# Three PSUM banks each for scores and transposed scores, with key sums moved behind the weighted product, in a differential-attention and gated-FFN kernel

## The chip, the cores and the metric

The kernel runs on one core of a Trainium2 chip. The metric is the device time of one execution in microseconds; times below are of the whole program, from the first to the last instruction unless said otherwise.

## The reference

The input is x, 16 batch elements of 1024 tokens with 256 features, float32. Cut to what matters:

```python
# x: (16, 1024, 256); H = 8 heads, D = 16, two score maps per head
n = layernorm(x)
q, k = xpos_rope(n @ Wq.T), xpos_rope(n @ Wk.T)     # 16 maps of depth 16
v = n @ Wv.T                                         # 8 heads of depth 32
probs = softmax(q @ k.T / 4)                         # 16 maps of 1024 x 1024
attn = (probs[:, 0] - lam * probs[:, 1]) @ v
x = x + (rms_norm(attn) * KEEP) @ Wo.T
n = layernorm(x)
c = scan over the batch: c = sigmoid(n@wf.T + c@uf.T + bf) * c
                           + sigmoid(n@wi.T + c@ui.T + bi) * tanh(n@wc.T + c@uc.T + bc)
out = x + tanh(n @ wo.T + c_final @ uo.T + bo)
```

The scan runs over the 16 batch elements, so the gates of one element need the cell state of the one before; the output needs the last cell state, so it is computed in a tail behind all elements.

## The kernel before, in words

The five engines run lists of instructions of their own and wait for each other's semaphores. The order on each engine is written out by hand. `iteration(b)` handles one batch element: the next element's queries and keys, the attention of two groups of four heads (attention 0 and attention 1), the mean squares and the output projection, the second normalisation, and the gates.

**Attention, in `attention`.** Each of the two attentions has 32 steps. In a step TensorE makes four transposed score tiles (`key_tile`, line 777: 128 keys by 512 queries of each of four heads, bf16, a row of the maxima added in the same product). ScalarE turns them into probabilities (`exps`, line 564). The probabilities are float32 and are used in two ways: the weighted product with the values (`weighted`, line 792, into `o_ps`), and the sums over the keys, the softmax denominators. For these POOL adds the probabilities of two successive steps (`pair`, line 472, one instruction per head), and TensorE multiplies the pair's sum by ones (`key_sums`, line 807, into `sum_ps`). Both products write 32 partitions per head, four heads side by side, and each shows as 8 matmuls. `weighted` of step s-1 stands in step s; `key_sums` of pair q, steps 2q and 2q+1, stands in step 2q+4.

**Scores.** The maxima that the softmax needs are taken from untransposed scores: 128 matmuls per attention (`score`, line 749), each into a bank `s_ps` of 512 float32, which VectorE reduces at once (`maximum`, line 1043). They belong to the *next* attention, and a plan (`score_plan`, from an assumed cost of the rotary work and of the sum steps) deals them out over the steps, 0 to 5 per step; 28 and 32 of them stand outside the steps, in the next queries and keys, the projections and the gates.

**PSUM.** It has eight banks. Before, `st[0]` and `st[1]` are two banks each and hold the transposed tiles of heads 0, 1 and 2, 3; `s_ps[0]`, `s_ps[1]` hold scores; `o_ps` and `sum_ps` have one each. A score waits until the maximum two before it is taken (line 748). A pair of tiles waits for the exp of the same half a step earlier (line 774). The ring of all other products (projections, mean squares, gates) goes through the four `st` banks in turn; `turn` is TensorE's wait for a free one, `take` ScalarE's read of it.

**VectorE** has, beside the maxima, the rotary embedding of the next queries and keys (`rope`, in the steps listed in `ROPE_AT`: the first nine and 13, 16 of attention 0; 5 to 10, 12, 13, 16, 20 of attention 1, here called the rotary steps), the turning and inversion of the key sums (`finish_sums`: for the last quarter of attention 0 it stands ahead of the first maximum in attention 1; for the others in steps 11, 19, 27 with `combine` a step later), and the normalisations.

**probs** is a ring of four steps. The exps of step s wait for `weighted` of step s-4 and, in even steps, for POOL's pair of steps s-4 and s-3 (lines 560, 561). POOL waits for all exps of both steps of its pair (line 466).

**Gates.** 12 gate tiles per element, each with a part from the old cell state and one from the normalised rows (line 891). Those of the first four tiles that need only the cell state stand ahead of the transposes of the second normalisation, whose statistics VectorE makes meanwhile (lines 983 to 1008).

The order inside a step, before:

```python
key_tile(u, g, s, 0)          # two tiles, heads 0 and 1
for i in todo[0:1]: score(un, 1 - g, i)
key_tile(u, g, s, 1)          # heads 2 and 3
for i in todo[1:2]: score(un, 1 - g, i)
if s >= 1: weighted(u, g, s - 1)
for i in todo[2:4]: score(un, 1 - g, i)
if s >= 4 and s % 2 == 0: key_sums(u, g, (s - 4) // 2)
for i in todo[4:]: score(un, 1 - g, i)
```

## Time and profile before

| what | us |
|---|---|
| median of three runs | 5261.81 (5261.59 to 5262.73) |
| the profiled execution | 5259.74 |
| its span, first to last instruction | 5257.9 |
| TensorE matmuls busy | 4979.5 (95%) |
| VectorE busy | 4021.4 (76%) |
| POOL busy | 2891.7 (55%) |
| ScalarE busy | 2722.8 (52%) |
| scores, line 749: 4096 matmuls | 1525.8 |
| transposed tiles, line 777: 4096 matmuls | 1226.9 |
| weighted product, line 792: 8192 matmuls | 1103.6 |
| key sums, line 807: 4096 matmuls | 543.4 |

One element takes about 313 us. Matmuls are pipelined and their ends are modelled, so TensorE's busy time overlaps itself; how far apart two matmuls start is the better measure of what each costs.

### The profile page before, as it was taken

Reading aid. Unit: us, or ns where it says so; the run is one execution under the profiler, and the core shown is the slowest. Engines: PE = TensorE matmul, PEld = TensorE weight load, DVE = VectorE, ACT = ScalarE, POOL = GpSimd, SP = SyncE. Lnnn points to the kernel's source line nnn. Section 1 sums busy time; section 2 is a strip of 40 time slices with the busy share of each in tenths; the row PEclk is TensorE's granted clock in tenths of the full one; section 3 lists DMA queues with packets and bytes.
Section 4 is the critical chain, followed back from the end, with each engine's and each line's share of the span. In section 5 each row is a group of like instructions: output and inputs, shape, how many; then the busy total and the mean of one; then the engine's idle time right before and its main releaser. Section 6 shows DMA issues by size and latency. Waiting matters only on the chain.

```text
span 5257.9 us, 65030 instructions
## 1 busy us (share of the span) xinstructions
PE 4979.5 (95%) x24784; PEld 1695.8 (32%) x24784; DVE 4021.4 (76%) x6183; ACT 2722.8 (52%) x3173; POOL 2891.7 (55%) x2118
## 2 busy tenths in 40 slices
PE   6999999999999999999999999999999999999999
PEld 2224232332423223242332423233242322323237
DVE  6877777877778877777887777787777887777526
ACT  1464645556465554545556454554546555463652
POOL 3573746647275573727657374664727557372750
PEclk7899999999999999999999999999999999999999
DMA  6031221302222131222303122130222213122117
GB/s 141 26 60 46 50 64 37 69 37 58 52 45 69 33 64 40 45 66 51 67 26 62 45 45 69 34 72 37 54 56 45 69 33 61 43 45 59 65 49 280
DMA packets 127706, 311.05 MB, mean 59 GB/s; under 512 B 27297, under 2 KB 30498, under 8 KB 113442
## 3 DMA queue, kind: packets, MB, share of 16 engines
q1 hardware_dynamic: 124178, 289.33, 23.2%
q10 hardware_dynamic: 3216, 17.57, 0.9%
q8 instruction: 195, 3.19, 0.3%
q14 instruction: 117, 0.96, 0.1%
HBM read 172.07 MB, written 99.61 MB: 52 GB/s over the span
## 4 chain that ended last, share of the span: by engine, by line
PE 64%; DVE 16%; issue 13%; POOL 3%; ACT 3%; DMA 0%; ACTq 0%; POOLq 0%; SPq 0%; DVEq 0%
PE o_ps L792 15%; PE s_ps L749 15%; PE st L777 13%; PE sum_ps L807 8%; DVE neg_max L1043 7%; PE st L891 3%; PE st L735 3%; POOL pair_sum L472 2%; PE st L717 2%; PE st L957 2%; ACT probs L564 2%; DVE stats L983 2%; DVE xa L1026 1%; DVE swapped L1021 1%; PE st L870 1%
## 5 line engine op out<-in xcount | busy, mean ns | idle before, releaser
L472 POOL TENSOR_TENSOR pair_sum<-probs 128x512 f32<-128x512 f32 x2048 | 2795.4, 1398 | 1436.4 <-ACT probs L564 1432.2
L1043 DVE TENSOR_REDUCE neg_max<-s_ps 128x1 f32<-128x512 f32 x4096 | 2679.4, 687 | 817.4 <-PE s_ps L749 810.1
L564 ACT ACTIVATE probs<-st 128x1024 f32<-128x1024 f32 x2048 | 1983.6, 1022 | 1240.9 <-PE st L777 996.0
L749 PE MATMUL s_ps<-k_stack,q_stack 96*128 96x512 bf16 x4096 | 1525.8, 393 | 140.9 <-DVE neg_max L1043 122.7
L777 PE MATMUL st<-q_stack,k_stack 99*128 99x512 bf16 x4096 | 1226.9, 385 | 20.2 <-ACT xa L512 6.6
L792 PE MATMUL o_ps<-probs,values 128*32 128x512 f32 x8192 | 1103.6, 611 | 0.7 <-ACT probs L564 0.7
L749 PEld LDWEIGHTS s_ps<-k_stack,q_stack 96*128 96x128 bf16 x4096 | 371.1, 97 | 1524.3 <-DVE neg_max L1043 1260.6
L777 PEld LDWEIGHTS st<-q_stack,k_stack 99*128 99x128 bf16 x4096 | 348.3, 99 | 792.6 <-ACT probs L564 414.8
L807 PE MATMUL sum_ps<-pair_sum,ones 128*32 128x512 f32 x4096 | 543.4, 602 | 7.7 <-POOL pair_sum L472 5.7
L891 PE MATMUL st<-xt,weights 128*128 128x512 f32 x768 | 381.7, 594 | 11.8 <-ACT xt L521 11.8
L891 PE MATMUL st<-cell_t,weights 128*128 128x512 f32 x768 | 362.9, 592 | 0.0
L512 ACT ACTIVATE probs<-st,gate_bias 128x512 f32<-128x512 f32 x192 | 131.6, 685 | 429.5 <-PE st L891 429.5
L792 PEld LDWEIGHTS o_ps<-probs,values 128*32 128x32 f32 x8192 | 161.9, 108 | 409.1 <-issue 381.3
L478 POOL TENSOR_TENSOR rstd<-var_eps,neg_half 128x8 f32<-128x8 f32 x18 | 29.6, 1647 | 433.5 <-DVE var_eps L1002 433.5
L717 PE MATMUL st<-xt,weights 128*128 128x512 f32 x512 | 248.1, 604 | 11.0 <-ACT xt L521 11.0
L1070 DVE STREAM_TRANSPOSE attn_t<-sum_ps 128x512 f32<-128x512 f32 x128 | 90.8, 709 | 184.7 <-PE sum_ps L807 184.7
L521 ACT ACTIVATE xt<-o_ps 128x512 f32<-128x512 f32 x64 | 38.2, 597 | 367.7 <-PE o_ps L704 367.6
L891 PEld LDWEIGHTS st<-xt,weights 128*128 128x128 f32 x768 | 144.6, 190 | 138.9 <-issue 113.3
L891 PEld LDWEIGHTS st<-cell_t,weights 128*128 128x128 f32 x768 | 144.6, 190 | 129.2 <-issue 120.8
L512 ACT ACTIVATE xa<-st 128x512 f32<-128x512 f32 x128 | 76.1, 597 | 208.1 <-PE st L717 199.9
L484 POOL TENSOR_TENSOR next_rstd<-var_eps,neg_half 128x8 f32<-128x8 f32 x14 | 22.9, 1636 | 273.2 <-DVE var_eps L1002 273.2
L807 PEld LDWEIGHTS sum_ps<-pair_sum,ones 128*32 128x32 f32 x4096 | 90.4, 108 | 219.2 <-issue 151.3
(129 smaller groups left out, 2980.3 us busy)
## 6 DMA issues: line engine op xcount, KB each, us to landing
q_stack<-qk_parts SPq DMA_DIRECT2D x384, 128.0 KB, 4.3
k_stack<-qk_parts SPq DMA_DIRECT2D x378, 128.0 KB, 7.0
swapped<-xa SPq DMA_DIRECT2D x128, 256.0 KB, 2.4
qk_parts<-swapped SPq DMA_DIRECT2D x64, 512.0 KB, 2.8
xa<-in_x SPq DMA_DIRECT2D x16, 1024.0 KB, 6.1
qk_parts<-low_part SPq DMA_DIRECT2D x64, 256.0 KB, 3.0
probs<-in_x SPq DMA_DIRECT2D x16, 1024.0 KB, 10.2
x_rows<-probs SPq DMA_DIRECT2D x16, 1024.0 KB, 3.9
```

What stands on the lines that cost most here:

```text
L472: pool.tensor_tensor(pair_sum[q % 2][:, h, :], probs[a % 4][:, h, :], probs[(a + 1) % 4][:, h, :], ALU.add)\
L512: act.activation(dst, ring(i), func, **kw).then_inc(act_out, 1)
L564: act.activation(probs[kk % 4][:, 2 * hp:2 * hp + 2, :], st[hp][:, :, :], ACT.Exp).then_inc(exp_done, 1)
L717: mm = pe.matmul(ring(i), weights[:, W_Q + X, c, g * P:(g + 1) * P], xt[:, c, h * HALF:(h + 1) * HALF], start=(c == 0), stop=(c == KC - 1))
L735: mm = pe.matmul(dst, src[:, c, at:at + P], weights[:, w, c, :], start=(c == 0), stop=(c == KC - 1))
L749: pe.matmul(s_ps[i % 2][:, :], q_stack[g][0:SROWS, s, t * P:(t + 1) * P], k_stack[g][0:SROWS, s, h * HALF:(h + 1) * HALF], start=True, sto ...
L777: mm = pe.matmul(st[hp][:, j, :], k_stack[g][0:KROWS, s, kt * P:(kt + 1) * P], q_stack[g][0:KROWS, s, th * HALF:(th + 1) * HALF], start=Tr ...
L792: mm = pe.matmul(o_ps[32 * h:32 * h + 32, :], values[:, kt, at:at + 2 * D], probs[kk % 4][:, h, :], start=(kt == 0), stop=(kt == KT - 1))
L807: mm = pe.matmul(sum_ps[32 * h:32 * h + 32, :], ones[:, 0:32], pair_sum[q % 2][:, h, :], start=(p == 0), stop=(p == 3))
L891: mm = pe.matmul(ring(GATE + i), weights[:, (U_F if cell else W_F) + a, c, ms], (cell_t if cell else xt)[:, c, hs], start=(start and c == ...
L957: mm = pe.matmul(ring(j)[:, t * E:(t + 1) * E], columns[:, at:at + P], weights[:, W_Z, c, :], start=(c == 0), stop=(c == KC - 1))
L1043: dve.tensor_reduce(neg_max2[:, at, i % 2:i % 2 + 1], s_ps[i % 2][:, :], AX.X, ALU.max, negate=True).then_inc(max_done, 1)
```

## The change

The eight banks are dealt out anew: three banks `st` of one tile each, three banks `s_ps`, and `o_ps`, `sum_ps` as before.

- `key_tile` makes one tile and waits for the exp three tiles before it; ScalarE runs one ACTIVATE of 512 columns per tile, 4096 instead of 2048 of 1024.
- A score waits for the maximum three before it.
- In a step the order is tile, score, tile, score, tile, weighted product, key sums, tile, the remaining scores.
- POOL waits per head for the exp of that head in the pair's second step.
- The ring of the other products has three banks; `turn` looks three places back. The bank follows from a count that goes on over the elements (`ring(rb + i)`, `bank`), and only three gates' cell parts stand ahead of the second transposes.
- In the tail the fourth bank is `s_ps[2]`.

```diff
-        st = [ctx.enter_context(nc.psum_tensor(f"st{i}", [P, 2, HALF], F32)) for i in range(2)]
-        s_ps = [ctx.enter_context(nc.psum_tensor(f"s_ps{i}", [P, HALF], F32)) for i in range(2)]
+        st = [ctx.enter_context(nc.psum_tensor(f"st{i}", [P, HALF], F32)) for i in range(BANKS)]
+        s_ps = [ctx.enter_context(nc.psum_tensor(f"s_ps{i}", [P, HALF], F32)) for i in range(BANKS)]
...
-        def ring(i):
-            return st[(i % 4) // 2][:, i % 2, :]
+        def ring(n):
+            return st[n % BANKS][:, :]
...
-                pool.wait_ge(exp_done, 64 * u + 4 * q + 4)
...
                 for h in range(4):
+                    pool.wait_ge(exp_done, TILES * u + 8 * q + 4 + (h + 1))
                     pool.tensor_tensor(pair_sum[q % 2][:, h, :], probs[a % 4][:, h, :],
...
-                    for hp in range(2):
-                        act.wait_ge(st_ready, 64 * u + (2 * kk + hp + 1))
-                        act.activation(probs[kk % 4][:, 2 * hp:2 * hp + 2, :], st[hp][:, :, :],
+                    for h in range(4):
+                        n = 4 * kk + h
+                        act.wait_ge(st_ready, TILES * u + n + 1)
+                        act.activation(probs[kk % 4][:, h, :], st[n % BANKS][:, :],
                                        ACT.Exp).then_inc(exp_done, 1)
...
-                p = i - 4
+                p = i - BANKS
...
-                if i >= 2:
-                    pe.wait_ge(max_done, SCORES * u + (i - 1))
-                pe.matmul(s_ps[i % 2][:, :], q_stack[g][0:SROWS, s, t * P:(t + 1) * P],
+                if i >= BANKS:
+                    pe.wait_ge(max_done, SCORES * u + (i - BANKS + 1))
+                pe.matmul(s_ps[i % BANKS][:, :], q_stack[g][0:SROWS, s, t * P:(t + 1) * P],
...
-            def key_tile(u, g, kk, hp):
+            def key_tile(u, g, kk, h):
...
+                n, s = 4 * kk + h, 2 * h + sub
+                if n >= BANKS:
+
+                    pe.wait_ge(exp_done, TILES * u + (n - BANKS + 1))
+                pe.matmul(st[n % BANKS][:, :], k_stack[g][0:KROWS, s, kt * P:(kt + 1) * P],
+                          q_stack[g][0:KROWS, s, th * HALF:(th + 1) * HALF],
+                          start=True, stop=True).then_inc(st_ready, 1)
...
-                    key_tile(u, g, s, 0)
-                    for i in todo[0:1]:
-                        score(un, 1 - g, i)
-                    key_tile(u, g, s, 1)
-                    for i in todo[1:2]:
-                        score(un, 1 - g, i)
+                    for h in range(2):
+                        key_tile(u, g, s, h)
+                        for i in todo[h:h + 1]:
+                            score(un, 1 - g, i)
+                    key_tile(u, g, s, 2)
                     if s >= 1:
                         weighted(u, g, s - 1)
-                    for i in todo[2:4]:
-                        score(un, 1 - g, i)
                     if s >= 4 and s % 2 == 0:
                         key_sums(u, g, (s - 4) // 2)
-                    for i in todo[4:]:
+                    key_tile(u, g, s, 3)
+                    for i in todo[2:]:
                         score(un, 1 - g, i)
...
-                for i in range(4):
+                for i in range(BANKS):
                     turn(GATE + i, b, ab)
                     gate_part(i, True, True, False)
                 transposes(xn2, ln2_out, b, 2 * b + (1 if last else 2))
```

## Rows read from the trace of the kernel before

**Rows 1.** The page, part 1: busy us, share of the span, instructions.

```profile
PE 4979.5 (95%) x24784; PEld 1695.8 (32%) x24784; DVE 4021.4 (76%) x6183; ACT 2722.8 (52%) x3173; POOL 2891.7 (55%) x2118
```

**Rows 2.** Timeline, two steps of attention 0: start, us, engine, line, what, count, [idle before].

```profile
2130.95 0.39 PE L749 MATMUL s_ps<-k_stack,q_stack 96*128 96x512 bf16 x1
2131.17 0.60 PE L777 MATMUL st<-q_stack,k_stack 99*128 99x512 bf16 x2
2131.37 1.99 DVE L1043 TENSOR_REDUCE neg_max<-s_ps 128x1 f32<-128x512 f32 x3 [0.24 <-PE s_ps L749]
...
2131.89 1.94 ACT L564 ACTIVATE probs<-st 128x1024 f32<-128x1024 f32 x2 [2.52 <-PE st L777]
...
2132.26 0.38 PE L749 MATMUL s_ps<-k_stack,q_stack 96*128 96x512 bf16 x1
...
2132.57 1.07 PE L792 MATMUL o_ps<-probs,values 128*32 128x512 f32 x8
...
2133.57 0.39 PE L749 MATMUL s_ps<-k_stack,q_stack 96*128 96x512 bf16 x1
...
2133.90 4.96 POOL L472 TENSOR_TENSOR pair_sum<-probs 128x512 f32<-128x512 f32 x4 [2.35 <-ACT probs L564]
```

**Rows 3.** Timeline, behind attention 1's last step, TensorE.

```profile
2275.97 1.06 PE L792 MATMUL o_ps<-probs,values 128*32 128x512 f32 x8
2276.85 1.04 PE L807 MATMUL sum_ps<-pair_sum,ones 128*32 128x512 f32 x8
2277.82 0.70 PE L735 MATMUL st<-weights,xt 128*128 128x256 f32 x2
```

**Rows 4.** Timeline, start of attention 1.

```profile
2174.04 1.88 DVE L1043 TENSOR_REDUCE neg_max<-s_ps 128x1 f32<-128x512 f32 x3
...
2174.78 0.39 PE L749 MATMUL s_ps<-k_stack,q_stack 96*128 96x512 bf16 x1 [2.68 <-DVE neg_max L1043]
```

**Rows 5.** Timeline, step 20 of attention 0, TensorE.

```profile
2121.95 0.39 PE L749 MATMUL s_ps<-k_stack,q_stack 96*128 96x512 bf16 x1 [0.28 <-DVE neg_max L1043]
...
2122.55 0.39 PE L749 MATMUL s_ps<-k_stack,q_stack 96*128 96x512 bf16 x1 [0.21 <-DVE neg_max L1043]
```

**Rows 6.** Timeline, behind a step of four scores, attention 0.

```profile
2126.71 0.60 PE L777 MATMUL st<-q_stack,k_stack 99*128 99x512 bf16 x2
...
2127.44 0.10 PEld L749 LDWEIGHTS s_ps<-k_stack,q_stack 96*128 96x128 bf16 x1 [0.63 <-DVE neg_max L1043]
```

**Rows 7.** Timeline, the rotary steps of the next element's attention 0.

```profile
2372.99 27.33 POOL L472 TENSOR_TENSOR pair_sum<-probs 128x512 f32<-128x512 f32 x16 [43.08 <-ACT probs L564]
...
2380.70 1.94 ACT L564 ACTIVATE probs<-st 128x1024 f32<-128x1024 f32 x2 [3.05 <-POOL pair_sum L472]
...
2381.78 0.60 PE L777 MATMUL st<-q_stack,k_stack 99*128 99x512 bf16 x2
```

**Rows 8.** Groups by line, ScalarE: count, busy us, mean ns, idle before, releasers.

```profile
L564 ACT ACTIVATE probs<-st 128x1024 f32<-128x1024 f32 x2048 | 1983.6, 1022 | 1240.9 <-PE st L777 996.0 <-POOL pair_sum L472 240.2 <-PE o_ps L792 2.1
...
L512 ACT ACTIVATE xa<-st 128x512 f32<-128x512 f32 x128 | 76.1, 597 | 208.1 <-PE st L717 199.9 <-issue 8.2
```

**Rows 9.** Timeline, gates' cell parts and the second transposes.

```profile
2302.19 7.03 PE L891 MATMUL st<-cell_t,weights 128*128 128x512 f32 x16
...
2309.96 0.65 PE L704 MATMUL o_ps<-ident,probs 128*128 128x128 f32 x4 [0.73 <-DVE probs L1008]
```

**Rows 10.** Windows at attention 1's start, two elements; the PEclk column is the granted clock.

```profile
2175.50:2178.90 3.40, 3.40 (x13) 0.55 (x11) 1.80 (x3) 2.05 (x2) 0.88 (x1) 0.50 1.09 145
...
4674.00:4677.40 3.40, 3.40 (x13) 0.57 (x11) 1.82 (x3) 2.05 (x2) 0.88 (x1) 0.50 1.09 145
```

**Rows 11.** Timeline, the last element's attention 1, TensorE's tiles.

```profile
5005.40 1.36 PE L777 MATMUL st<-q_stack,k_stack 99*128 99x512 bf16 x4
...
5010.51 1.36 PE L777 MATMUL st<-q_stack,k_stack 99*128 99x512 bf16 x4
```

**Rows 12.** Timeline, the first scores of element 0's attention 1, VectorE.

```profile
161.94 13.83 DVE L1043 TENSOR_REDUCE neg_max<-s_ps 128x1 f32<-128x512 f32 x20 [0.77 <-PE s_ps L749]
```

More of the change, by code:

```diff
@@ L47 @@
 SCORES = SUBS * TT * 2
+BANKS = 3
+TILES = 4 * STEPS
 def act_index(i):
@@ L94, with ring_base @@
 NO_PLAN = [range(0)] * STEPS
+def ring_base(b, last):
+    return b * PER_ITER + (PRE - (PRE if last else 0))
 def build(nc, x, wq, wk, wv, wo_attn, lq1, lk1, lq2, lk2, wf, uf, bf, wi, ui, bi, wc, uc, bc,
@@ L170, in build @@
         gee_ps = [o_ps, sum_ps, s_ps[0], s_ps[1]]
-        def ring(i):
-            return st[(i % 4) // 2][:, i % 2, :]
+        def ring(n):
+            return st[n % BANKS][:, :]
+        tail_ps = [ring(ring_base(NB - 1, True) + GEE + j) for j in range(3)] + [s_ps[2][:, :]]
         first_in = sem("first_in")
@@ L236, in build @@
         block = ctx.enter_context(nc.Block())
-        def ring_base(b, last):
-            return b * PER_ITER + (PRE - (PRE if last else 0))
         def act_base(b, last):
@@ L339, in iteration @@
                     sp.wait_ge(x2_out, 16 * NB)
-                    sp.wait_ge(st_ready, 64 * (u + 1))
+                    sp.wait_ge(st_ready, TILES * (u + 1))
                     for s in range(4):
@@ L356, in iteration @@
                 if last:
-                    sp.wait_ge(st_ready, 64 * (u + 2))
+                    sp.wait_ge(st_ready, TILES * (u + 2))
                     for s in range(4, SLOTS):
@@ L511, in take @@
                 act.wait_ge(ring_ready, rb + i + 1)
-                act.activation(dst, ring(i), func, **kw).then_inc(act_out, 1)
+                act.activation(dst, ring(rb + i), func, **kw).then_inc(act_out, 1)
             def take_xt(n):
@@ L692, in turn, with bank @@
                     pe.wait_ge(act_out, ab + (act_index(p) + 1))
+            def bank(i, b, ab):
+                return ring(ab + (PER_ITER - ACT_ITER) * b + i)
             def transposes(src, ln_out, m, n, blocks=iter(())):
@@ L716, in qk @@
                         for c in range(KC):
-                            mm = pe.matmul(ring(i), weights[:, W_Q + X, c, g * P:(g + 1) * P],
+                            mm = pe.matmul(bank(i, b, ab), weights[:, W_Q + X, c, g * P:(g + 1) * P],
                                            xt[:, c, h * HALF:(h + 1) * HALF],
@@ L731, in rows_out @@
                     for t in range(2):
-                        dst = ring(i)[:, t * E:(t + 1) * E]
+                        dst = bank(i, b, ab)[:, t * E:(t + 1) * E]
                         at = (2 * j + t) * P
@@ L767, in turn_max @@
                     .then_inc(max_turned, 1)
[L769 removed]
+            def key_tile(u, g, kk, h):
                 th, sub, kt = kk // 16, kk // 8 % 2, kk % 8
[L772 to L781 removed]
+                n, s = 4 * kk + h, 2 * h + sub
[4 more added lines that the diff above has]
+                          start=True, stop=True).then_inc(st_ready, 1)
             def weighted(u, g, kk):
                 r, kt = kk // 8, kk % 8
[L786 removed]
+                pe.wait_ge(exp_done, TILES * u + 4 * (kk + 1))
                 if kt == 0 and (g == 1 or r > 0):
@@ L869, in mean_square @@
                     turn(squares_at[i], b, ab)
-                    pe.matmul(ring(squares_at[i]), head_ones[:, :], square[:, i, :], start=True,
+                    pe.matmul(bank(squares_at[i], b, ab), head_ones[:, :], square[:, i, :], start=True,
                               stop=True).then_inc(ring_ready, 1)
@@ L890, in gate_part @@
                     for c in range(KC):
-                        mm = pe.matmul(ring(GATE + i),
+                        mm = pe.matmul(bank(GATE + i, b, ab),
                                        weights[:, (U_F if cell else W_F) + a, c, ms],
@@ L910, in iteration @@
                 pe.wait_ge(xt_out, 4 * (2 * b + (2 if last else 3)))
-                for i in range(4):
+                for i in range(BANKS):
                     gate_part(i, False, False, True).then_inc(ring_ready, 1)
-                for i in range(4, 12):
+                for i in range(BANKS, 12):
                     if i == 5 and not last:
@@ L949, in z_rows @@
                 for j in range(4):
-                    if k == 0:
+                    if k == 0 and j < 3:
                         turn(GEE + j, NB - 1, act_base(NB - 1, True))
-                    else:
+                    if k > 0:
                         pe.wait_ge(tail_add, 4 * (k - 1) + (j + 1))
@@ L956, in z_rows @@
                             at = c * T + (2 * j + t) * P
-                            mm = pe.matmul(ring(j)[:, t * E:(t + 1) * E], columns[:, at:at + P],
+                            mm = pe.matmul(tail_ps[j][:, t * E:(t + 1) * E], columns[:, at:at + P],
                                            weights[:, W_Z, c, :], start=(c == 0),
@@ L1170, in iteration @@
                     dve.wait_ge(ring_ready, rb + (WO + j + 1))
-                    dve.tensor_tensor(rows, ring(WO + j), rows, ALU.add).then_inc(wo_added, 1)
+                    dve.tensor_tensor(rows, ring(rb + WO + j), rows, ALU.add).then_inc(wo_added, 1)
                     if j == 1:
@@ L1261, in _ @@
                     dve.wait_ge(tail_z, 4 * k + (j + 1))
-                    dve.tensor_tensor(tail_n[k % 6][:, rows], ring(j), x2[:, rows], ALU.add)\
+                    dve.tensor_tensor(tail_n[k % 6][:, rows], tail_ps[j], x2[:, rows], ALU.add)\
                        .then_inc(tail_add, 1)
```

14 lines of the change are left out of this document (2 added, 12 removed).

## The prediction

> **What bounds the kernel now.** I read the page's busy shares first [rows 1]: TensorE is busy 95% of the span, VectorE 76%, POOL 55%, ScalarE 52%. That alone doesn't say that TensorE bounds each stretch, so I went on to the timeline. In a plain step of the attention [rows 2] every bf16 matmul of 512 columns follows the one before at 0.22 us and nothing is idle, except around the 32-column f32 groups: a weighted product or key sum starts 0.31 us after the matmul ahead of it (2132.26 to 2132.57), 0.09 more than the 0.22, and the next starts 1.00 later (2132.57 to 2133.57). Where key sums already follow a weighted product directly [rows 3], they start after 0.88 and are done after 0.97. So the pair costs 2 x (0.09 + 1.00) = 2.18 us apart and 0.09 + 0.88 + 0.97 = 1.94 together: a joined group saves 0.24 us of TensorE. Elsewhere TensorE stands, and the rows name who holds it: VectorE [rows 4 to 6], POOL [rows 7]. It follows that a saving counts only where neither of these binds.
>
> One batch element has two attentions of 32 steps. The step plan (worked out from its constants) gives, in attention 0, scores per step 3 2 1 2 3 1 3 2 5 1 5 0 5 1 5 4 2 4 5 0 4 4 5 3 5 3 5 0 5 3 5 4, and in attention 1, 3 3 4 3 5 1 3 2 2 2 3 0 2 1 5 3 3 4 4 0 3 3 5 3 5 3 5 0 4 3 5 4. The first 15 elements are alike; the last has no scores in its attention 1.
>
> **Joined key sums.** Of the 14 in each attention, 13 and 12 have scores ahead of them now. Five (attention 0, steps 4, 6, 8; attention 1, steps 6, 10) lie where POOL binds (below) and save nothing. 20 x 0.24 = -4.8 us per element.
>
> **Scores in one burst.** The price is that third, fourth and fifth score now stand together behind the fourth tile, with the next step's first two right behind. VectorE starts 0.42 us after a score does (2130.95 to 2131.37), takes 0.69 and, back to back, 0.60 each (1.88 for 3) [rows 4]; a score follows a freed bank after 0.04 (2174.04 + 0.69 to 2174.78). With three banks the next step's first score needs the maximum of the third score: 0.42 + 0.69 + 0.04 = 1.15 us after it, while its slot comes at 4 x 0.22 = 0.87: a stall of 0.28; the second one stalls a further 0.17 (0.42 + 0.69 + 0.60 + 0.04 = 1.75 against 1.15 + 2 x 0.22). After five scores, where two or more follow (steps 14, 22, 24, 28, 30 and 14, 22, 24, 30), this is 9 x 0.45; where one follows, 2 x 0.28; after four, 6 x 0.07: +5.0 us. So the third bank doesn't buy the join; together they are worth nothing.
>
> **What the third score bank takes away.** In a step of four scores the one at 2127.44 comes 0.30 after its slot (2126.71 + 2 x 0.22) [rows 6]; five such steps, -1.5. In steps 19 and 20 of attention 0 VectorE turns the sums and two scores wait, 0.28 and 0.60 - 0.22 [rows 5]; with a bank more and the joined sums ahead of them, -0.7. At the start of attention 1 a score waits 2.68 us for the last sums' turning [rows 4]; now one score and one tile get ahead of that wait: -0.5.
>
> **Three tile banks, one tile per ACTIVATE.** ScalarE starts 0.50 us after the last tile of a pair does (2131.17 + 0.22 to 2131.89). A 512 copy out of PSUM takes 597 ns, a 1024 exp 1022, two of them 1.94 [rows 2, 8]: so a 512 exp should take about 0.60, and 0.49 back to back. A tile's matmul follows its exp by 0.06 (2380.70 + 1.02 to 2381.78) [rows 7]. The round trip is 0.50 + 0.60 + 0.06 = 1.16 us. Third tile and weighted product need the exp of the step before's fourth tile, which is now issued behind the f32 groups. Between the two lie 3 slots and the scores: with two scores 5 x 0.22 = 1.08, so 0.07 late; with one 0.29; with none 0.51. Outside POOL's stretches this gives +1.3 us per element, less an estimated 0.1 in each of the six steps without scores, whose weighted product waits for a 1.02 us exp now and for a 0.60 one then: +0.7. ScalarE itself gets 4 x 0.49 = 1.96 us per step against at least 2.17 of TensorE, so it doesn't bind by its load. I take the copy's 0.60 for the exp; the bounds are 0.49, as if only the pitch counted, and as much above, 0.71, which is 2 us per element either way.
>
> The Trainium skill, "VectorE: DVE Perf Modes", section "The TRN2 errata — SBUF-src ops pay a fixed extra latency per instruction", speaks against the split: each ScalarE instruction out of PSUM pays 172 cycles beside its elements, which I estimate at 0.14 us, or 290 us of ScalarE more for 2048 more instructions. By its formula a 512 exp takes 0.57 us; the sum would be some 0.5 us per element lower than by the row's 0.60. The trace agrees in size (1.02 for 1024).
>
> **POOL starts per head.** Now it starts a pair when both steps' exps are all done, 2.73 us after the step's first tile (2131.17 to 2133.90). Now the first tile's exp suffices, at 1.16: up to 1.5 us earlier. This counts only where POOL binds: beside the rotary steps its 16 additions take 27.33 us, 1.71 each against 1.24 in a plain stretch (4.96 for 4), and ScalarE waits for it, first 3.05 us [rows 2, 7]. POOL then works without a pause, so the whole stretch ends earlier by what it starts earlier: an estimated 1.4 in attention 0 and 1.2 in attention 1, taken just under the 1.5; bounds 0 and 3.0: -2.6 us.
>
> **The ring of 3 in the gates.** Only three gates' cell parts instead of four stand ahead of the second normalisation. The four take 16 matmuls of 0.43, 6.9 us from 2302.19, and TensorE then waits 0.73 more for VectorE [rows 9]. One part, 4 x 0.43 = 1.72, goes out from under this cover and is paid behind it. The output projection's scores wait less, which brings the additions ahead of the statistics forward by at most 0.44: +1.3 us.
>
> **The clock.** After the 2.68 us wait the granted clock is 0.50, 1.2 GHz, from 2175.5 to 2178.9, and so it is at this place in the four elements of which I asked, the first and last of them shown [rows 10]. The wait shrinks to about 2.3; but the idle ahead of the second normalisation's transposes grows from 0.9 to about 3. I take a loss of 1.2 us in most elements there and half the 1.4 of the other place back: +0.3; bounds -1.4 to +1.5.
>
> **Sum of an element:** -4.8 + 5.0 - 1.5 - 0.7 - 0.5 + 0.7 - 2.6 + 1.3 + 0.3 = -2.8 us; 15 of them -42.
>
> **Last element.** Its attention 0 has no rotary work: join 13 x -0.24, bursts +3.1, the rest -0.9: -0.9. The gates +1.7. Its attention 1, without scores, has two steps in 5.11 us now, TensorE taking 1.36 or 1.04 for four tiles [rows 11]. With three banks the third tile waits the whole 1.16, then 0.31 + 1.00 until the fourth: 2.43, and 0.86 more with key sums: 5.72 us for two. 16 x 0.61 = +9.6. Together +10.
>
> **Start.** The first 156 scores run at 1.2 GHz mostly, where two banks give 13.83 us for 20, 0.69 each, with VectorE waiting for the next score [rows 12]; three banks give VectorE's 0.60. Some 125 scores x 0.095 = -12 us.
>
> The sum is -44 us against the profiled execution's own 5259.7 us (span 5257.9), which lies 2 below the median of 5261.8: **5218 us**, 0.8% faster. A measurement of this kernel tells about 0.2%, 10 us, from no change.
>
> **Rivals.**
> - *Only the waits go, the bursts cost nothing* (VectorE and TensorE interleave better than I count, say because small stalls merge): 5.0 x 16 = 80 us less of cost at most, half of it likely: some 5180 us. For: TensorE's stalls don't add where ScalarE's and VectorE's coincide. Against: the 1.15 us are read from rows. Chance 0.17.
> - *The fourth tile's round trip decides, and it becomes slower.* It is 1.16 us against 1.08 of cover in 19 steps per element and 1.30 in ten. Each 0.1 us more costs 1.9 us, then 2.9, per element. From +0.1 (1.26) on, 28 us of the gain are gone; at +0.16 the change is even; with 0.3 more the element pays 0.3 x 19 + 0.16 x 10 = 7.3 us: that is 5218 + 109 = 5327 us. For: it is paid at every step. Against: both ends of it stand in rows. Chance 0.18.
> - *Gains and losses cancel:* POOL's earlier start isn't passed on, since its additions beside VectorE's rotary work just stretch (-2.6 gone, 39 us): 5257 us. Chance 0.17.
> - *My sum*: 0.48, own range 5195 to 5245.
>
> Of these, below 5251 lie my sum, the first rival and a little of the others. The range of 8 in 10 reaches from 5175 to 5280. Faster 0.68, the same 0.13, slower 0.19.
>
> **What would show it.** Per step: key sums 0.88 us behind a weighted product everywhere; scores behind a five-score burst 0.28 and 0.17 late, with VectorE as releaser; the third tile waiting for ScalarE in steps with few scores; ScalarE's exps at 0.60 us, 4096 of them; POOL's first addition 1.2 us after the first tile; the wait at attention 1's start at 2.3; TensorE idle about 3 us ahead of the second transposes, with a half-clock stretch behind it; two steps of the last attention in 5.7 us. The prediction is wrong if the 512 exp takes over 0.7, if POOL's additions get longer as they start earlier, or if the bursts' stalls are absent.

## The result: slower by 1.4%

The changed kernel takes 5341.13 us, median of four runs (5301.62, 5327.91, 5354.35, 5354.43), against 5261.7 (5259.78 to 5262.73) for the kernel before: ratio 1.014, interval 1.0115 to 1.0165. Forecast were 5218 us and a range of 5175 to 5280. The profiled execution of after is the 5301.62 one (span 5299.8), 41.9 us above that of before.

Busy time and the costliest groups of after, from its page (columns as in [rows 1, 8]):

```profile
PE 4985.9 (94%) x24784; PEld 1734.7 (33%) x24784; DVE 3910.6 (74%) x6183; ACT 2926.7 (55%) x5221; POOL 2887.9 (54%) x2118
...
L570 ACT ACTIVATE probs<-st 128x512 f32<-128x512 f32 x4096 | 2199.5, 603 | 1054.2 <-PE st L785 968.4
L758 PE MATMUL s_ps<-k_stack,q_stack 96*128 96x512 bf16 x4096 | 1477.2, 391 | 85.2 <-DVE neg_max L1047 60.3
L785 PE MATMUL st<-q_stack,k_stack 99*128 99x512 bf16 x4096 | 1487.0, 386 | 30.9 <-ACT probs L570 11.6
L798 PE MATMUL o_ps<-probs,values 128*32 128x512 f32 x8192 | 1098.4, 608 | 13.2 <-ACT probs L570 8.5
...
L813 PE MATMUL sum_ps<-pair_sum,ones 128*32 128x512 f32 x4096 | 537.2, 596 | 47.8 <-POOL pair_sum L477 25.0
```

The same groups of before, from the grouped view:

```profile
L749 PE MATMUL s_ps<-k_stack,q_stack 96*128 96x512 bf16 x4096 | 1525.8, 393 | 140.9 <-DVE neg_max L1043 122.7 <-DVE shift L1063 1.4
L777 PE MATMUL st<-q_stack,k_stack 99*128 99x512 bf16 x4096 | 1226.9, 385 | 20.2 <-ACT xa L512 6.6 <-ACT probs L564 4.2 <-DMA q_stack<-shift 1.0
L792 PE MATMUL o_ps<-probs,values 128*32 128x512 f32 x8192 | 1103.6, 611 | 0.7 <-ACT probs L564 0.7
L807 PE MATMUL sum_ps<-pair_sum,ones 128*32 128x512 f32 x4096 | 543.4, 602 | 7.7 <-POOL pair_sum L472 5.7
```

TensorE's idle time ahead of scores fell by 56 us; ahead of key sums it rose by 40, ahead of weighted products by 12, ahead of tiles by 11. Idle time counts only what goes beyond a matmul's modelled end (0.39 us, at a pitch of 0.22). Start against start it reads differently; the pitches are the prediction's, 0.22 us between bf16 matmuls and 0.31, 1.00 and 0.88 around the f32 groups. Over the two attentions of an element (mean of 15), the slots that the new order needs without any wait are 4.92 us shorter (25 joins, less a tile's slot that now falls into each span; the prediction's join term was 4.8); scores come 1.56 us later behind their slots, tiles 0.47, weighted products 1.17 and key sums 3.98, in all +2.26 us. So the join saved what it should, and more than half of what was lost stands ahead of the key sums themselves.

Where the time went shows best in the intervals between the first matmuls of successive weighted products (there are 1024 of them). "Step s" below is the interval from the weighted product in step s to the next one, a mean over 15 elements, after less before.

| part, us | before | after | difference |
|---|---|---|---|
| start to the first weighted product | 185.9 | 176.2 | -9.7 |
| attention 0, first to last product | 100.33 | 100.57 | +0.24 |
| attention 0 to attention 1 | 16.78 | 15.26 | -1.52 |
| attention 1 | 98.94 | 100.97 | +2.03 |
| to the next element | 96.13 | 98.42 | +2.29 |
| last element's attention 1 | 78.24 | 88.10 | +9.9 |

**A five-score step.** TensorE, ScalarE and VectorE of after, from the timeline of attention 1's end, step 30 and, in the last row, the product behind step 31; the later fences of this kind have the same columns as [rows 2]:

```profile
2279.01 1.07 PE L798 MATMUL o_ps<-probs,values 128*32 128x512 f32 x8
...
2279.89 1.04 PE L813 MATMUL sum_ps<-pair_sum,ones 128*32 128x512 f32 x8
...
2280.87 0.39 PE L785 MATMUL st<-q_stack,k_stack 99*128 99x512 bf16 x1
...
2281.09 0.81 PE L758 MATMUL s_ps<-k_stack,q_stack 96*128 96x512 bf16 x3
2281.29 0.60 ACT L570 ACTIVATE probs<-st 128x512 f32<-128x512 f32 x1 [1.39 <-PE st L785]
2281.51 3.08 DVE L1047 TENSOR_REDUCE neg_max<-s_ps 128x1 f32<-128x512 f32 x5 [1.60 <-PE s_ps L758]
...
2281.74 0.38 PE L785 MATMUL st<-q_stack,k_stack 99*128 99x512 bf16 x1
...
2282.26 0.39 PE L758 MATMUL s_ps<-k_stack,q_stack 96*128 96x512 bf16 x1
...
2282.86 0.39 PE L758 MATMUL s_ps<-k_stack,q_stack 96*128 96x512 bf16 x1
...
2285.47 1.07 PE L798 MATMUL o_ps<-probs,values 128*32 128x512 f32 x8 [0.25 <-ACT probs L570]
```

The joined sums stand 0.88 behind the product, as forecast. The next step's first score comes at 2282.26, 0.52 after the tile ahead of it instead of 0.22: 0.30 late; the second 0.37 after its tile: 0.15 late (forecast 0.28 and 0.17). The last row was not foreseen: behind step 31's fourth tile (in no other step) a weighted product waits for the exp of that same step's fourth tile. Step 31 is 0.54 longer in each attention.

**The sums that open a quarter** (steps 12, 20, 28). After, step 20 of attention 0 (the place of [rows 5]):

```profile
2127.26 1.07 PE L798 MATMUL o_ps<-probs,values 128*32 128x512 f32 x8
2127.47 0.70 DVE L1094 TENSOR_TENSOR sum_ps<-o_copy,sum_ps 128x512 f32<-128x512 f32 x1
2128.28 0.75 DVE L1103 SCALAR_TENSOR_TENSOR attn_t<-sum_ps,neg_lam,o_copy 128x512 f32<-128x512 f32 x1
...
2129.18 1.06 PE L813 MATMUL sum_ps<-pair_sum,ones 128*32 128x512 f32 x8 [0.86 <-POOL pair_sum L477]
```

```profile
2118.93 4.96 POOL L477 TENSOR_TENSOR pair_sum<-probs 128x512 f32<-128x512 f32 x4 [1.89 <-ACT probs L570]
```

The sums of a new quarter write the bank `sum_ps` that VectorE still reads for the last quarter. Its reading ends at 2129.03; the key sums, ready at 2128.14, start at 2129.18. The row blames POOL's pair sum, but POOL had this pair ready at 2123.89 (second fence), 5 us earlier; by the code the first product of a quarter also waits for VectorE's reading, whose end lies 0.15 ahead of the start. In attention 1 the row names VectorE itself:

```profile
2218.45 1.06 PE L798 MATMUL o_ps<-probs,values 128*32 128x512 f32 x8
2221.03 1.07 PE L813 MATMUL sum_ps<-pair_sum,ones 128*32 128x512 f32 x8 [1.52 <-DVE o_copy L1091]
```

**Ahead of the second transposes** (the place of [rows 9]), and the granted clock behind them (PEclk) in this element and two others:

```profile
2310.95 5.32 PE L895 MATMUL st<-cell_t,weights 128*128 128x512 f32 x12
2318.80 0.66 PE L713 MATMUL o_ps<-ident,probs 128*128 128x128 f32 x4 [2.53 <-DVE probs L1012]
```

```profile
2320.50:2327.30 6.80, 6.11 (x15) 2.91 (x14) 0.71 (x2) 3.00 (x5) 0.00 (x0) 0.50 0.37 154
743.50:750.30 6.80, 6.11 (x15) 2.89 (x14) 0.69 (x1) 2.98 (x5) 0.00 (x0) 0.50 0.38 157
4528.90:4535.70 6.80, 5.98 (x14) 3.09 (x15) 0.69 (x1) 2.95 (x4) 0.00 (x0) 0.50 0.37 154
```

TensorE idles 2.53 us instead of 0.73, and then works at 1.2 GHz. It does so for 6.83 us in 11 of 15 elements and for 3.41 us in a twelfth, though the idle is 2.53 or 2.54 us in all 15. What such a stretch costs stands in the same trace: of the elements 0 to 13, the two without it take 96.47 us from attention 1's last product to the next element's first, the eleven with 6.83 us of it 98.92 to 99.36. All half-clock stretches together are 247 us, 224 before.

### The profile page after: what moved, and what is told of

Its sections match the earlier page's. It is cut to its first block, busy times and chain, and to the rows that moved or that the text cites. A ratio compares the mean times of both kernels' runs of the same rounds, so it can differ in the third digit from the quotient of the medians.

```text
span 5299.8 us, 67078 instructions
## 1 busy us (share of the span) xinstructions
PE 4985.9 (94%) x24784; PEld 1734.7 (33%) x24784; DVE 3910.6 (74%) x6183; ACT 2926.7 (55%) x5221; POOL 2887.9 (54%) x2118
## 4 chain that ended last, share of the span: by engine, by line
PE 72%; DVE 17%; ACT 4%; POOL 4%; issue 2%; DMA 0%; ACTq 0%; POOLq 0%; SPq 0%; DVEq 0%
PE o_ps L798 15%; PE st L785 14%; PE s_ps L758 14%; PE st L895 11%; DVE neg_max L1047 8%; PE sum_ps L813 8%; PE st L726 4%; POOL pair_sum L477 3%; ACT probs L570 2%; PE st L744 2%; PE st L961 2%; DVE xa L1030 1%; DVE swapped L1025 1%; PE st L874 1%; DVE stats L987 1%
## 5 line engine op out<-in xcount | busy, mean ns | idle before, releaser
L1047 DVE TENSOR_REDUCE neg_max<-s_ps 128x1 f32<-128x512 f32 x4096 | 2596.6, 683 | 959.2 <-PE s_ps L758 957.6
L570 ACT ACTIVATE probs<-st 128x512 f32<-128x512 f32 x4096 | 2199.5, 603 | 1054.2 <-PE st L785 968.4
L758 PE MATMUL s_ps<-k_stack,q_stack 96*128 96x512 bf16 x4096 | 1477.2, 391 | 85.2 <-DVE neg_max L1047 60.3
L785 PE MATMUL st<-q_stack,k_stack 99*128 99x512 bf16 x4096 | 1487.0, 386 | 30.9 <-ACT probs L570 11.6
L785 PEld LDWEIGHTS st<-q_stack,k_stack 99*128 99x128 bf16 x4096 | 377.4, 98 | 1303.3 <-ACT probs L570 819.2
L758 PEld LDWEIGHTS s_ps<-k_stack,q_stack 96*128 96x128 bf16 x4096 | 402.6, 98 | 789.1 <-DVE neg_max L1047 431.8
L895 PE MATMUL st<-xt,weights 128*128 128x512 f32 x768 | 400.4, 619 | 11.1 <-ACT xt L526 11.1
L726 PE MATMUL st<-xt,weights 128*128 128x512 f32 x512 | 249.0, 606 | 30.5 <-ACT xa L517 19.3
L813 PEld LDWEIGHTS sum_ps<-pair_sum,ones 128*32 128x32 f32 x4096 | 118.8, 109 | 386.6 <-issue 228.6
```

Source lines behind the costliest of these rows:

```text
L570: act.activation(probs[kk % 4][:, h, :], st[n % BANKS][:, :], ACT.Exp).then_inc(exp_done, 1)
L726: mm = pe.matmul(bank(i, b, ab), weights[:, W_Q + X, c, g * P:(g + 1) * P], xt[:, c, h * HALF:(h + 1) * HALF], start=(c == 0), stop=(c == ...
L758: pe.matmul(s_ps[i % BANKS][:, :], q_stack[g][0:SROWS, s, t * P:(t + 1) * P], k_stack[g][0:SROWS, s, h * HALF:(h + 1) * HALF], start=True, ...
L785: pe.matmul(st[n % BANKS][:, :], k_stack[g][0:KROWS, s, kt * P:(kt + 1) * P], q_stack[g][0:KROWS, s, th * HALF:(th + 1) * HALF], start=Tru ...
L813: mm = pe.matmul(sum_ps[32 * h:32 * h + 32, :], ones[:, 0:32], pair_sum[q % 2][:, h, :], start=(p == 0), stop=(p == 3))
L895: mm = pe.matmul(bank(GATE + i, b, ab), weights[:, (U_F if cell else W_F) + a, c, ms], (cell_t if cell else xt)[:, c, hs], start=(start an ...
```

## The experiments

All with the interval against the kernel before, in the same session. "Filled" means the changed kernel with the edit of the first experiment: it takes away the half clock behind the second transposes and most of the scatter, so that small edits can be told apart.

**1. The gap behind the gates' cell parts filled.** Two more products, whose results nobody reads, in the bank `s_ps[2]` behind the three cell parts:

```diff
+                if not last:
+                    pe.wait_ge(max_done, SCORES * (u + 2) + SCORES - LATE[4] - 2 + 1)
+                for c in range(KC):
+                    pe.matmul(s_ps[2][:, :], weights[:, U_F, c, 0:P], cell_t[:, c, 0:HALF],
+                              start=(c == 0), stop=(c == KC - 1))
```

> The changed kernel, with four further cell-state passes (two products of 512 columns, 1.72 us, into the bank s_ps[2], read by nobody) behind the three gates' cell parts, so that TensorE is busy ahead of the second transposes as it was before. Theory 1, the clock: the idle 2.5 us there is what brings the 6.8 us of half clock in most elements; filled, they go, and the time falls by 13 x 2.6 = 34 us from the profiled 5302 to about 5268, and from the slower executions (5328, 5354) to the same 5268, so that the spread goes too. Theory 2, the moved part alone: the clock has other causes; the filler hides under the wait and the time stays at 5302 to 5354 with its spread.

Measured: 5282.0 us (5276.0 to 5282.48; the kernel adds work and leaves none out), ratio 1.0036 (1.0023 to 1.0049). Timeline, and the granted clock behind the transposes:

```profile
2305.87 1.88 PE L916 MATMUL s_ps<-cell_t,weights 128*128 128x512 f32 x4
2308.56 0.66 PE L713 MATMUL o_ps<-ident,probs 128*128 128x128 f32 x4 [0.81 <-DVE probs L1017]
```

```profile
2310.00:2316.80 6.80, 6.06 (x23) 3.17 (x24) 2.84 (x5) 3.78 (x6) 0.00 (x0) 1.00 0.38 157
```

More work and 59 us less than after's median (20 less than its profiled execution): the idle was dear through the clock. Without a half-clock stretch the way to the next element is the same with and without the two products (96.46 and 96.47 us), so they cost and save nothing else there. The runs now lie 6 us apart instead of 53. 20 us stay that the clock doesn't explain, on top of the savings that should have come.

**2. The three cell parts alone,** in the kernel before:

```diff
-                for i in range(4):
+                for i in range(3):
                     turn(GATE + i, b, ab)
                     gate_part(i, True, True, False)
...
-                for i in range(4):
+                for i in range(3):
                     gate_part(i, False, False, True).then_inc(ring_ready, 1)
-                for i in range(4, 12):
+                for i in range(3, 12):
```

> The kernel before, with only three gates' cell parts ahead of the second transposes (four banks kept). Theory 1, part moved and clock lost: 16 x 1.7 = 27 us for the moved part and up to 15 x 2.6 = 39 us for the clock: 5289 to 5328. Theory 2, only the moved part: 5289. Rival: the wait was there anyway and nothing changes, 5262.

Measured: 5295.27 us, ratio 1.0064 (1.0049 to 1.0079). The way to the next element is 98.84 us against 96.13: +2.7, where the prediction had +1.3 for the gates and +0.3 for the clock; the way to attention 1 is 0.6 shorter. 15 x 2.1 is 31 of the total's 33 us. Elements without half clock take 97.64 us against 95.92 in the kernel before: here the moved part costs its whole 1.72. TensorE idles 2.45 us ahead of the transposes in all 15 elements, but only four then show 6.83 us of half clock and one 3.41: the idle alone doesn't decide whether the clock falls.

**3. The join alone,** in the kernel before, with its two score banks:

```diff
                     if s >= 1:
                         weighted(u, g, s - 1)
-                    for i in todo[2:4]:
-                        score(un, 1 - g, i)
                     if s >= 4 and s % 2 == 0:
                         key_sums(u, g, (s - 4) // 2)
-                    for i in todo[4:]:
+                    for i in todo[2:]:
```

> The kernel before, with the key sums directly behind the weighted product and nothing else (two score banks, pairs of tiles). The prediction's join term: 0.24 us in 20 places of an element, 72 us, less bursts of three scores on two banks: each third score waits some 0.5 us more in ten steps, 75 us, so about even, 5262. Rival from the trace after: the sums that open an accumulation (steps 12, 20, 28) now wait for VectorE's reading of sum_ps, some 1 us in step 20 and 0.2 in others, 1.5 us per element more, 5285.

Measured: 5411.68 us, ratio 1.0285 (1.0268 to 1.0302), worse than both theories had it. Behind a join of this kernel:

```profile
2342.97 1.04 PE L807 MATMUL sum_ps<-pair_sum,ones 128*32 128x512 f32 x8
2343.95 0.61 PE L749 MATMUL s_ps<-k_stack,q_stack 96*128 96x512 bf16 x2
2345.12 0.39 PE L749 MATMUL s_ps<-k_stack,q_stack 96*128 96x512 bf16 x1 [0.57 <-DVE neg_max L1041]
```

With two banks the burst's third score waits for VectorE. The key sums had been the cover between two pairs of scores.

**4. POOL waits for the whole pair again,** in the changed kernel:

```diff
+                pool.wait_ge(exp_done, TILES * u + 8 * q + 8)
...
-                    pool.wait_ge(exp_done, TILES * u + 8 * q + 4 + (h + 1))
```

> The changed kernel, with POOL waiting for all exps of its pair again. The prediction's term: POOL binds beside the rotary work, 2.6 us per element: 39 us slower, 5341 to 5393 by execution. Rival from the trace after: VectorE's own chain binds attention 1's rotary steps (11.6 us from the fifth rotary product to the reading of the sums in both kernels) and POOL's start is worth 1 us at most, in attention 0: up to 15 us slower.

Measured: 5338.59 us, ratio 1.0147 (1.0132 to 1.0162). The total can't be set against after's scattered runs (298 us at half clock here, 247 in after's profile). The intervals can: attention 0 is 0.94 longer; attention 1 is 0.24 longer, but in none of its rotary steps (0.13 in the first step, where the half clock falls, 0.10 in step 21). POOL's early start is worth 0.9 per element, not 2.6. Of this run, whose granted clock was 0.972, there is a trace: it has 6.83 us of half clock behind the second transposes in all 15 elements, and 3.41 at the start of nearly every attention 1.

**5. Two score banks in the new order,** filled:

```diff
-                if i >= BANKS:
-                    pe.wait_ge(max_done, SCORES * u + (i - BANKS + 1))
-                pe.matmul(s_ps[i % BANKS][:, :], ...
+                if i >= 2:
+                    pe.wait_ge(max_done, SCORES * u + (i - 1))
+                pe.matmul(s_ps[i % 2][:, :], ...
...
-                dve.tensor_reduce(neg_max2[:, at, i % 2:i % 2 + 1], s_ps[i % BANKS][:, :], AX.X,
+                dve.tensor_reduce(neg_max2[:, at, i % 2:i % 2 + 1], s_ps[i % 2][:, :], AX.X,
```

> The filled kernel (5282) with scores in two banks again, everything else as changed. Theory 1: the third score bank pays for most of what the burst costs; on two banks the third score of a burst waits 1.15 - 0.43 = 0.7 us after the first, as the joined key sums on the kernel before did (0.50 us net more in each five-score step): 2 x 10 steps x 0.5 and more per element, 150 us, about 5430. Theory 2, by the prediction's bookkeeping (the bank gives back only 1.5 + 0.7 + 0.5 us per element): 40 us, 5322.

Measured: 5576.08 us, ratio 1.0598 (1.0582 to 1.0614). The third bank carries the new order: without it 294 us more.

**6. The third score ahead of the weighted product,** filled. The join stays:

```diff
+                    for i in todo[2:3]:
+                        score(un, 1 - g, i)
                     if s >= 1:
                         weighted(u, g, s - 1)
...
-                    for i in todo[2:]:
+                    for i in todo[3:]:
```

> The filled kernel (5282) with the third score of a step ahead of the weighted product, behind the third tile, so that at most two stand together behind the fourth tile. Theory 1, bursts: the 0.23 us more that each five-score step shows in the trace (0.47 of stall less the join's 0.24) go in nine steps of an element, and 0.2 in two more: 9 x 0.40 + 0.4 = 4 us, 60 us, to 5222. Theory 2, VectorE's throughput: the stall is only moved to the next score that needs a bank; 5282.

Measured: 5201.24 us, ratio 0.9885 (0.9868 to 0.9901); 81 us below the filled kernel, and below what the theory had. Its five-score step:

```profile
2233.12 0.39 PE L785 MATMUL st<-q_stack,k_stack 99*128 99x512 bf16 x1
2233.35 0.60 PE L758 MATMUL s_ps<-k_stack,q_stack 96*128 96x512 bf16 x2
2233.78 0.38 PE L785 MATMUL st<-q_stack,k_stack 99*128 99x512 bf16 x1
2234.00 0.38 PE L758 MATMUL s_ps<-k_stack,q_stack 96*128 96x512 bf16 x1
```

Behind a burst of two the next step's first score stands in its slot; only the two behind it come late, by 0.07 and 0.15, and such steps are 0.22 shorter. The moved score also gives VectorE work earlier and the opening sums more cover: step 12 is 0.71 and 0.99 shorter, step 20 of attention 0 0.68.

**7. The opening sums behind the fourth tile and two scores,** filled; all other key sums stay joined:

```diff
-                    if s >= 4 and s % 2 == 0:
+                    sums = s >= 4 and s % 2 == 0
+                    if sums and s % 8 != 4:
                         key_sums(u, g, (s - 4) // 2)
                     key_tile(u, g, s, 3)
-                    for i in todo[2:]:
+                    for i in todo[2:4]:
+                        score(un, 1 - g, i)
+                    if sums and s % 8 == 4:
+                        key_sums(u, g, (s - 4) // 2)
+                    for i in todo[4:]:
```

> The filled kernel (5282) in which only the key sums that open an accumulation (steps 12, 20, 28) stand behind the fourth tile and two scores, the others where the change puts them. Theory 1, the wait for sum_ps: TensorE waits 1.0 us for VectorE's reading in step 20 of attention 0, 1.5 in step 12 of attention 1 and 0.2 to 0.5 elsewhere; behind the tile and the scores this is covered, less the 0.24 of the join: 1.5 to 2.5 us per element, 23 to 38 us, to 5245 to 5259. Theory 2: VectorE's rotary chain binds there whatever stands in TensorE's list, and only step 20 gains 0.8 us per element: 5270.

Measured: 5259.85 us (ten runs, 5255.59 to 5279.08), ratio 1.0002 (0.9993 to 1.0012), at the upper edge of the theory's figure: 22 us come back. Some 13 of them are the edit's: 0.9 us per element, over all steps but attention 1's first. That one is 0.3 shorter too, where the two kernels differ only in the half clock. Step 20 of attention 0 gains nothing: where the key sums came 1.04 us late, the scores ahead of them now come 1.01 late. In attention 1, step 12, the wait does not vanish:

```profile
2202.63 0.39 PE L785 MATMUL st<-q_stack,k_stack 99*128 99x512 bf16 x1
2204.20 1.06 PE L813 MATMUL sum_ps<-pair_sum,ones 128*32 128x512 f32 x8 [1.19 <-DVE o_copy L1101]
```

There VectorE's chain is the bound, and moving the sums by itself doesn't end the wait. In experiment 6, where the chain starts earlier, it is 0.51, with both edits (experiment 9) 0.18.

**8. The join alone undone,** filled: the fourth tile and two scores between the weighted product and all key sums:

```diff
                     if s >= 1:
                         weighted(u, g, s - 1)
+                    key_tile(u, g, s, 3)
+                    for i in todo[2:4]:
+                        score(un, 1 - g, i)
                     if s >= 4 and s % 2 == 0:
                         key_sums(u, g, (s - 4) // 2)
-                    key_tile(u, g, s, 3)
-                    for i in todo[2:]:
+                    for i in todo[4:]:
                         score(un, 1 - g, i)
```

> The filled kernel with the join alone undone: the fourth tile directly behind the weighted product, then third and fourth score, then the key sums, then the fifth score; three banks of each kind stay. Theory (the join brings little by itself, and its place costs): undone, 24 groups cost 0.24 more (+5.8 us per element), but the burst stalls (-5.0), the opening sums' wait for VectorE (-1.7), step 31's wait for the fourth exp (-1.1) and the copy's delay (-0.5) go: -2.5 us per element, 5282 - 38 = 5244 us. Rival (the join pays for itself, the losses come from elsewhere): 5282 + 15 x 5.8 less the opening sums' wait = 5345 us.

Measured: 5239.39 us, ratio 0.9958 (0.9941 to 0.9974). The new banks without the join beat the kernel before; with the join in the place that it has they don't (5282). Key sums now come 0.4 us late per element in all, against 4.3 in the filled kernel.

**9. Experiments 6 and 7 together, and in step 31 the fourth tile ahead of the weighted product,** filled:

```diff
+                    if s == STEPS - 1:
+                        key_tile(u, g, s, 2)
+                        key_tile(u, g, s, 3)
+                        weighted(u, g, s - 1)
+                        for i in todo[2:]:
+                            score(un, 1 - g, i)
+                        continue
```

> The filled kernel (5282) with both: third score ahead of the weighted product, opening key sums late, and in the last step of an attention the fourth tile ahead of the weighted product (step 31 shows 0.54 us more than before in each attention). If the terms add: 60 + 23 to 38 + 15 = about 100 us, 5180, and so 80 faster than the kernel before. If they overlap, since VectorE and TensorE are both near full: half of it, 5230.

Measured: 5184.64 us (5181.2 to 5189.77), ratio 0.9856 (0.9841 to 0.987): 1.4% faster than the kernel before. Step 31 is 0.54 shorter in each attention. The 97 us below the filled kernel are near the expected 100, but not by its terms: experiment 6 alone gave 81 and step 31 gives 16 (15 x 1.08), so the late opening sums add nothing on top of the moved score.

**10. The same without the filling products.**

> The kernel with all three orders repaired, but without the two filling products behind the gates' cell parts. If the idle ahead of the second transposes costs the granted clock by itself, as the filler over the changed kernel showed (59 us between 5341 and 5282), it should come back: half-clock stretches 137 us behind attention 1's first weighted product in most elements, about 240 to 260 us at half clock against 187, and some 5184.6 + 59 = 5244 us, with a wide spread between runs. If the clock was a matter of the whole element's load, which the repaired orders have raised, it stays at about 5184.6 less the filler's own work of 15 x 0.86 us at most: 5172 to 5190.

Measured: 5224.02 us (5221.75 to 5226.08), ratio 0.9929 (0.9915 to 0.9944). Timeline, and the granted clock behind it:

```profile
2282.39 0.66 PE L713 MATMUL o_ps<-ident,probs 128*128 128x128 f32 x4 [2.54 <-DVE probs L1026]
```

```profile
2283.80:2290.60 6.80, 6.09 (x14) 3.18 (x15) 0.69 (x1) 2.84 (x4) 0.00 (x0) 0.50 0.37 154
```

The same idle (2.54 us) and the same 6.83 us at 1.2 GHz, now in all 15 elements, each 131 or 132 us behind attention 1's first weighted product. The way to the next element is 99.09 us against 96.24 filled; 15 x 2.85 is 43 us, and the whole difference is 39.4. The theory had 59 and a wide spread: the price was 2/3 of that, and the spread did not come back. So such a stretch costs 2.85 us here, and 2.5 to 2.9 in after's trace.

## Why the prediction was wrong

Right were the prices read from rows: 0.24 for a join (steps 18 and 26 are 0.24 shorter), 0.45 of stall behind a five-score step (0.30 + 0.15; such a step, less the join, is 0.23 longer), the 512 exp (603 ns against 0.60), the start (-9.7 against -12), and the last element's attention 1 (+9.9 against +9.6; two steps 5.66 against 5.72). For these two steps the rows give 1.08 where the prediction had 1.16 for the way from the fourth tile over its exp to the next step's third tile. It also slipped twice in adding: 1.16 + 0.31 + 1.00 is 2.47 and not 2.43, and 16 x 0.61 is 9.8. With 2.47 it would have had 5.80. The rows:

```profile
5042.24 1.07 PE L798 MATMUL o_ps<-probs,values 128*32 128x512 f32 x8
5043.24 0.82 PE L785 MATMUL st<-q_stack,k_stack 99*128 99x512 bf16 x3
5044.32 0.39 PE L785 MATMUL st<-q_stack,k_stack 99*128 99x512 bf16 x1 [0.26 <-ACT probs L570]
```

By the formula that the prediction took from the Trainium skill, "VectorE: DVE Perf Modes", section "The TRN2 errata — SBUF-src ops pay a fixed extra latency per instruction", that exp would take 0.57 us; the trace has 603 ns, and the measurement decides.

Wrong were four steps in the attentions. For the two attentions of an element the forecast's terms sum to -3.9 us; measured +2.3 (0.24 + 2.03), a gap of 6.2. What each step of the forecast missed is read from the intervals, less the forecast's own terms for that place:

- **"With a bank more and the joined sums ahead of them, -0.7."** The step looked at who waits behind the sums, and not at what the sums wait for: the bank that VectorE still reads. Steps 19 and 20 of attention 0 measured +0.08 together, where the forecast's terms give -0.87. The other opening steps outside attention 1's rotary stretch (12 and 28 of attention 0, 20 and 28 of attention 1) are 0.2 longer each than their terms. That is 1.8 us. In experiment 8 these waits go, but for 0.4 us in step 12 of attention 1, and step 20 is 0.67 shorter though its join is undone. Experiment 7 ends them for the sums only: in step 20 the scores then wait for the same stretch of VectorE.
- **POOL starts per head, -2.6.** The largest miss: 2.7 us. The stretch of attention 1 was not POOL's. From a rotary sum to the end of the turned sums VectorE works without a pause and takes 14.95 us before (2197.84 to 2212.79) and 14.98 after (2205.82 to 2220.80), so the 1.49 won in step 10 came back as 1.94 in step 12. VectorE's first and last rows of that chain, before:

```profile
2197.84 2.32 DVE L1026 TENSOR_TENSOR xa<-xa,swapped 128x1024 f32<-128x1024 f32 x1
...
2212.79 1.28 DVE L1043 TENSOR_REDUCE neg_max<-s_ps 128x1 f32<-128x512 f32 x2
```

  after:

```profile
2202.59 0.69 DVE L1047 TENSOR_REDUCE neg_max<-s_ps 128x1 f32<-128x512 f32 x1 [1.38 <-PE s_ps L758]
...
2205.82 2.32 DVE L1030 TENSOR_TENSOR xa<-xa,swapped 128x1024 f32<-128x1024 f32 x1
...
2220.80 1.28 DVE L1047 TENSOR_REDUCE neg_max<-s_ps 128x1 f32<-128x512 f32 x2
```

  Ahead of it VectorE idles 1.38 us for a score that the new order makes late; that fits with what a score moved forward gives here (experiment 6, step 12), but no run changed this idle alone. In intervals: attention 0's steps 1 to 8 are 0.7 shorter instead of 1.4, attention 1's steps 4 to 13 are 1.1 longer instead of 1.2 shorter, of which 0.25 is the copy's (below): 0.7 + 2.0. Experiment 4 shows what of the forecast's 2.6 was POOL's: 0.9, all in attention 0. The third rival had it (the earlier start not passed on), but by another mechanism: POOL's 16 additions in attention 1's stretch take 26.3 us after (12.85 + 13.43) and 26.8 before, so they don't stretch. By the code, step 12's key sums follow the weighted product directly in both kernels (two scores only), so the join has no part in its +1.94.
- **Step 31.** That a last weighted product needs the same step's fourth tile stood in the code and not in the prediction: 0.54 twice, 1.1 us; experiment 9, with the fourth tile ahead of the product, took exactly that away.
- **The copy of `o_ps`.** ScalarE copies the finished quarter behind the fourth exp, which is late now. The product that opens the bank waits for it:

```profile
2118.45 1.07 PE L798 MATMUL o_ps<-probs,values 128*32 128x512 f32 x8 [0.18 <-ACT o_copy L548]
```

  Step 16 of attention 0 and step 8 of attention 1 are 0.25 longer, and the forecast had nothing for them: with two scores each, their key sums stood directly behind the weighted product before as well. That is 0.5 us. In experiment 8, with the fourth tile earlier, the wait is gone from the rows, and the undone join takes its place: the steps stay as long.

Together 6.1 of the 6.2; the rest isn't placed. The fourth tile's round trip, the second rival, didn't become slower: third tiles come 1.0 us late per element in all, 1.6 before, and in the last attention the trip takes 1.08 us. Its 5327 us come near the result for a reason that isn't its own.

**The clock** is the fifth. Taken was +0.3 us per element. In the profiled execution gates, clock and attention 1's start together came to +0.8 (2.29 - 1.52), against 1.3 + 0.3 - 0.5 = +1.1. That the sum held is luck: without half clock the way to the next element is 96.47 us after and 95.92 before, so the gates' moved part cost 0.55 with the other changes and not 1.3, while 11 of 15 elements paid 2.5 to 2.9 for the clock and not 1.2. And that is after's fastest run. The median lies 39.5 us above it, with a granted clock of 0.970 to 0.974 against 0.977, and experiment 1 took 59 us off it. The prediction had the idle (about 3 us; 2.53) and the half clock behind it, and priced that at 1.2 us; experiment 10 shows 2.85 for 6.83 us at half speed. Since only the fastest run has a trace, where each half-clock stretch falls in the slower ones stays open; experiment 4, nearly the same kernel, had it in all 15 elements at a granted clock of 0.972.

The sum was -44 us and the profiled execution's difference is +41.9, 85.9 apart. The attentions' terms are 93 of it (6.2 x 15), gates, clock and attention 1's start -5, start and last element with the tail together -2 (+2.3 and -4.1). The further 39.5 to the median go with the lower granted clock; no trace of those runs shows more.

Whether the three changes were each worth it: the third score bank saves 294 us in this order (5 against 1), and the join costs 43 where it was put (8 against 1). The place of one score is worth 81 us (6 against 1). With it the kernel is faster than without the join (5201 against 5239), but these two differ in two things, and the kernel with the moved score and without the join wasn't run: whether the join pays there isn't shown.

## What to carry to other kernels

Before a product is moved forward, list what it waits for itself, in each of its kinds (the first of a quarter, the last of a loop), and not only who waits behind it; the first and last of a series have waits that the middle doesn't show. When a stretch has a bound, follow every engine's chain through it: taking away the first stall moves it to the engine that is next. An idle of some 2.5 us on TensorE between dense stretches can cost more than itself, as here through the clock, and two products of no use in it made this kernel faster.

## What the runs showed of the hardware

- A TensorE idle of 2.53 us was followed by 6.83 us of granted clock 0.50 (1.2 GHz) in 11 of 15 elements (3.41 us in one more); one of 2.54, in the kernel of experiment 10, in 15 of 15; one of 2.45, in that of experiment 2, in 4 of 15 (3.41 us in one more); one of 0.81, with two products put in, in none at this place. Such a stretch of 6.83 us cost 2.5 to 2.9 us.
- Two products more per element, of no use to the result (four records, 1.88 us), made the program 59 us shorter in the median, and its runs agree within 6.5 us instead of 53.
- A 512-column exp out of PSUM takes 603 ns alone and 0.49 us more for each back to back (1.57 us for three, from 2278.32), where one of 1024 takes 1022 ns. Splitting 2048 instructions in two added 216 us of ScalarE's busy time (1983.6 to 2199.5).
